# The down product of a spline-weight feed-forward layer: quarters of outputs, segment sums, and a reordered residual

## What is computed

```python
x = layernorm(x + attention(x))                    # 16 heads of 32, low-rank factors
x = layernorm(x + x * decayed_running_sum(ctx*ctx))
gate_w = spline(gate_cp, 2048, 512)                # cubic in 8134 control points,
up_w   = spline(up_cp, 2048, 512)                  # read out at out*in positions
down_w = spline(down_cp, 512, 2048)
inter = silu(x @ gate_w.T) * (x @ up_w.T)          # 2048 hidden units
x = layernorm(x + inter @ down_w.T)                # the down product
```

## Time and profile before

| | us |
|---|---|
| median of 3 runs (669.69 to 670.2) | 669.72 |
| the profiled execution | 670.12 |
| its span, first to last instruction | 668.3 |
| PE busy in it | 648.3 (97%) |
| feed-forward block 0, gate matmul to gate matmul (366.38 to 448.62) | 82.24 |
| blocks 1 and 2, each | 71.0 |
| from the last index' gate matmul to the end | 16.5 |

### The profile page before, as it was taken

How to read it: one execution, slowest core, us unless ns; L and a number is a source line. 1 busy time by engine, 2 the same in 40 slices (tenths; PEclk the granted TensorE clock), 3 DMA queues, 4 the chain that set the end, 5 groups by cost and what they waited for, 6 DMA issues and landing times.

```text
span 668.3 us, 12061 instructions
## 1 busy us (share of the span) xinstructions
PE 648.3 (97%) x4312; PEld 532.6 (80%) x4312; DVE 421.9 (63%) x790; ACT 360.5 (54%) x1038; POOL 291.5 (44%) x351
## 2 busy tenths in 40 slices
PE   8999999999999999999988799999999999999995
PEld 8687888878888788887856577888888888888884
DVE  3465686768777677776777788666554555454434
ACT  5566665656657676676776556552333333333222
POOL 0746389797747768585654936100010001000102
PEclk9999999999999999999998999999999999999998
DMA  9612020030220422021123662742183416440301
GB/s 328 225 59 96 1 95 1 2 127 1 60 99 2 137 75 69 7 74 43 42 66 71 157 166 69 209 104 46 32 232 78 100 32 184 92 103 0 127 1 63
DMA packets 22268, 58.07 MB, mean 87 GB/s; under 512 B 4033, under 2 KB 7233, under 8 KB 21313
## 3 DMA queue, kind: packets, MB, share of 16 engines
q1 hardware_dynamic: 17296, 45.50, 23.3%
q0 software_dynamic: 4624, 11.28, 5.6%
q10 hardware_dynamic: 288, 0.52, 0.3%
HBM read 32.11 MB, written 8.39 MB: 61 GB/s over the span
## 4 chain that ended last, share of the span: by engine, by line
PE 90%; DVE 4%; ACT 4%; issue 1%; POOL 0%; DVEq 0%; POOLq 0%; ACTq 0%
PE bank L303 22%; PE bank L305 21%; PE bank L304 21%; PE bank L490 8%; PE bank L478 5%; PE bank L512 5%; PE bank L1216 2%; PE bank L1121 2%; ACT probs L679 2%; PE bank L498 1%; PE bank L529 1%; PE bank L402 1%; PE bank L316 1%; PE bank L1190 1%; ACT hidden_hi_lo L1394 1%
## 5 line engine op out<-in xcount | busy, mean ns | idle before, releaser
L679 ACT ACTIVATE probs<-bank,minus_max 128x256 f32<-128x256 f32 x256 | 118.6, 488 | 38.8 <-DVE minus_max L847 38.6
L847 DVE TENSOR_REDUCE minus_max<-bank 128x2 f32<-128x512 f32 x128 | 79.5, 683 | 46.3 <-PE bank L478 46.3
L303 PE MATMUL bank<-down,hidden_hi_lo 128*128 128x512 f32 x256 | 100.8, 394 | 1.5 <-DVE hidden_hi_lo L1427 1.5
L304 PE MATMUL bank<-down,hidden_hi_lo 128*128 128x512 f32 x256 | 99.9, 390 | 0.0
L305 PE MATMUL bank<-down,hidden_hi_lo 128*128 128x512 f32 x256 | 99.8, 390 | 0.0
L1381 ACT ACTIVATE silu<-bank 128x512 f32<-128x512 f32 x64 | 38.3, 598 | 80.7 <-PE bank L305 79.9
L1423 DVE TENSOR_TENSOR hidden<-bank,silu 128x512 f32<-128x512 f32 x64 | 44.1, 690 | 59.5 <-PE bank L305 57.3
L858 DVE COPY probsT<-bank 128x512 f32<-128x512 f32 x96 | 59.9, 679 | 19.7 <-PE bank L490 19.6
L1427 DVE TENSOR_TENSOR hidden_hi_lo<-hidden,hidden_hi_lo 128x512 fp32r<-128x512 f32 x64 | 45.6, 712 | 40.8 <-ACT hidden_hi_lo L1394 40.7
L1394 ACT CAST hidden_hi_lo<-hidden 128x512 fp32r<-128x512 f32 x64 | 39.7, 621 | 52.7 <-DVE hidden L1423 52.7
L1498 POOL TENSOR_TENSOR ffn_var_eps<-ffn_mean_var,constants 128x4 f32<-128x4 f32 x3 | 0.6, 199 | 154.9 <-DVE ffn_mean_var L1443 154.9
(11 more groups left out here) (172 smaller groups left out, 1610.8 us busy)
## 6 DMA issues: line engine op xcount, KB each, us to landing
features_by_group<-features_by_cell SPq DMA_DIRECT2D x128, 128.0 KB, 2.3
ctx_squared_T<-in_ctxT SPq DMA_DIRECT2D x8, 512.0 KB, 6.2
xres<-in_x SPq DMA_DIRECT2D x8, 512.0 KB, 4.6
x_in<-x SPq DMA_DIRECT2D x16, 256.0 KB, 2.9
x_residual<-x POOLq DMA_DIRECT2D x4, 1024.0 KB, 6.7
xin_T<-in_xT SPq DMA_DIRECT2D x7, 512.0 KB, 4.0
x<-x_rows SPq DMA_DIRECT2D x7, 512.0 KB, 4.3
out_x<-x_residual POOLq DMA_DIRECT2D x12, 256.0 KB, 3.0
```

The source lines that it names most:

```text
L303: nc.tensor.matmul(out, wh, xh, start=first, stop=False)
L304: nc.tensor.matmul(out, wh, xl, start=False, stop=False)
L679: inc(nc.scalar.activation(probs[:, g, t, :], S[g][:, t * T:(t + 1) * T], ACT.Exp, bias=nmax[:, g, t:t + 1], accum_out=rsum[:, t, g:g + 1] ...
L847: inc(nc.vector.tensor_reduce(nmax[:, g, :], S[g][:].rearrange("p (t k) -> p t k", t=TT), AX.X, ALU.max, negate=True), "max")
```

## The change

Hidden units and outputs are both cut into Q = 4 quarters. A unit's position in every down row is its own number, so a unit lies close to the knots of some rows only. Quarters are chosen so that outside a quarter's own outputs the units can be joined to 16 segments that hold no knot of the other outputs' rows.

- `pe_raw`: the product of a quarter's 64 units of an index with its own 128 outputs, exactly. Two quarters lie on the partitions 0 to 63 and 64 to 127 of an index: six matmuls of 64 rows, in alternation into two banks. Results are now transposed: outputs on the partitions, 512 tokens as columns.
- `pe_moments`: two full matmuls for an index with the constant `by_segment` gather four moments of each segment into bank Mo. Twice in a block ACT and DVE split Mo into high and low, and `pe_polynomials` multiplies them with `down_by_moment` into all four banks (12 matmuls).
- One pair of units is moved between two quarters to make them equal; three more matmuls of 64 rows correct for it.
- `act_outs` and `dve_outs` copy the four banks out, `pe_outs` turns them back with 16 transposes, and the residual is added with 16 instructions for each pair of token tiles, because the residual's columns are sorted otherwise than those of the sum (`column_order`; x, context, Wo, decay and out_x are permuted on the host).
- A step is now two indices of a pair of quarters (st = 0 to 7); a feature group is used at st = g // 2 and again at 4 + g // 2. The turns, the jobs, the adds, and the statistics get new places; the norm goes from DVE to ACT (`act_out`) with its factors from POOL.
- The down jobs are 13 instead of 32, with 8 matmuls of 256 columns each instead of 2, ten of them in the first five indices of block 0. Their makers (426 KB with the mask, for each job) are rounded by two POOL DMAs from DRAM to DRAM in batches 2 and 3 and come in by 13 DMAs that SP issues, in four buffers.

```diff
+        k = i - 2 * NG
+        pe.wait_ge(s_mkd[k % 4], 16 * (k // 4 + 1))
+        mk = mk_dn[k % 4][:, 0:OUT_MAKER].rearrange("p (c h m) -> p c h m", c=2, h=2)
+        pieces = out[:].rearrange("p (e m) -> p e m", e=2)
+        if k == STEPS:
+            for piece in range(2):
+                for of, coef in ((0, 0), (1, piece)):
+                    for h in range(2):
+                        last = nc.tensor.matmul(out[:, piece * GROUP:piece * GROUP + P], mk[:, of, h, 0:P],
+                                                downD[:, h, coef, P:2 * P], start=of == h == 0, stop=of == h == 1)
+            inc(last, "w")
+            return
+        for cb in range(2):
+            for b in range(2):
+                q = 2 * (k // Q) + b if k < STEPS else 2 * ((k - STEPS - 1) % 2) + cb
+                for h in range(2):
+                    last = nc.tensor.matmul(pieces[:, :, cb * P:(cb + 1) * P], mk[:, cb, h, b * PART:b * PART + P],
...
+    def sp_makers_out(sp, k):
+        if k == 0:
+            sp.wait_ge(s["mkc"], 32)
+            sp.wait_ge(s["mkm"], 16)
+        if k < 3:
+            wait(sp, "v", 2 * B)
+        elif k == 3:
+            wait(sp, "o", 2 * B)
+        else:
+            wait(sp, "ws", 2 * NG + k - 3)
+        sp.dma_start(mk_dn[k % 4][:].bitcast(F32), makers_d2[k].bitcast(F32)).then_inc(s_mkd[k % 4], 16)
+
+    def pool_round_makers(pool, part):
+        at = slice(7 * part, min(7 * part + 7, DJOBS))
+        inc(pool.dma_start(makers_d2[at, :, 0:OUT_MAKER], makers_out_d[at, :, 0:OUT_MAKER]), "mkc", 16)
...
+    def pe_moments(pe, n, st, j):
+        pair, pr = divmod(st, Q)
+        pe.wait_ge(s["hl"], index(n, st, j) + 1)
+        if pr == j == 0:
+            wait(pe, "mol", 2 * n + pair)
+            if n == st == 0:
+                wait(pe, "ws", AHEAD_JOBS)
+                pe.wait_ge(s["seg"], 16)
+        for h in range(2):
+            last = nc.tensor.matmul(Mo[:], by_segment[:, JT * st + j, :], hid[:, st % 2, h, j, :],
+                                    start=pr == h == j == 0, stop=pr == Q - 1 and h == j == 1)
+        if pr == Q - 1 and j == 1:
+            inc(last, "mo")
...
+    def pe_raw(pe, n, st, j):
+        pair, pr = divmod(st, Q)
...
+        if pr == j == 0:
+            if n == pair == 0:
+                wait(pe, "r1", 2 * B)
+            elif n == 0:
+                pe.wait_ge(s["ws"], NJOB)
+            elif pair == 0:
+                wait(pe, "yqa", 2 * n - 1)
+                wait(pe, "yqd", 2 * n - 1)
+            else:
+                wait(pe, "add", 2 * n)
+        for k, (lo_w, lo_h) in enumerate(((0, 0), (0, 1), (1, 0))):
+            for b in range(2):
+                rows_ = slice(b * PART, (b + 1) * PART)
+                last = nc.tensor.matmul(Dn[2 * pair + b][:], raw[st][rows_, lo_w, j * P:(j + 1) * P],
+                                        hid[rows_, st % 2, lo_h, j, :], start=pr == j == k == 0, stop=False)
+        if st == MOVED_STEP and j == 0:
+            pe.wait_ge(s["hused"], index(n, st, j))
+            for lo_w, lo_h in ((0, 0), (0, 1), (1, 0)):
+                last = nc.tensor.matmul(Dn[1][:], raw[STEPS][0:PART, lo_w, 0:P], hid[0:PART, st % 2, lo_h, 0, :],
+                                        start=False, stop=False)
+        inc(last, "hused")
...
+    def pe_polynomials(pe, n, pair):
+        pe.wait_ge(s["mol"], 2 * n + pair + 1)
+        if n == 0:
+            wait(pe, "wld", STEPS + 2 * pair)
+        for q in range(Q):
+            last = three(Dn[q][:], [by_poly[:, pair, h, q * P:(q + 1) * P] for h in range(2)], [mom[:, pair, h, :] for h in range(2)],
+                         False, pair == 1)
+            inc(last, "d" if pair else "kap")
+
...
+
+    def pe_outs(pe, n, t):
...
-            wait(pe, "rs1", 2 * B)
-        elif g == 0:
-            wait(pe, "add", BT * (n - 1) + t + 1)
+            pe.wait_ge(s["yqa"], 2 * n + 2)
+            pe.wait_ge(s["yqd"], 2 * n + 2)
+        elif t == 2 and n < NB - 1:
+            pe.wait_ge(s["add"], 2 * n + 1)
+        for q in range(Q):
+            last = nc.tensor.transpose(Dn[outs_bank(n, t)][:, q * P:(q + 1) * P], yq[:, q, t * P:(t + 1) * P], ident[:])
+        inc(last, "pm")
...
+    def jobs_of(n, st, j):
+
+        first = AHEAD_JOBS + 2 * index(n, st, j)
+        return range(first, min(first + 2, NJOB)) if n == 0 else ()
+
...
+            pe_gate_up(pe, n, st, j)
+            pe_turn(pe, n, st, j, 0)
+            pe_fill(pe, n, st, j)
+            if n and st == 1 and j == 0:
+                pe_polynomials(pe, n - 1, 1)
+            if st:
+                pe_moments(pe, n, st - 1, j)
+                pe_raw(pe, n, st - 1, j)
+            elif n:
+                pe_moments(pe, n - 1, STEPS - 1, j)
+                pe_raw(pe, n - 1, STEPS - 1, j)
+            if st == 5 and j == 1:
+                pe_polynomials(pe, n, 0)
+            if n and (st, j) == (1, 1):
+                pe_outs(pe, n - 1, 0)
+                pe_outs(pe, n - 1, 1)
+            if n and (st, j) == (2, 1):
+                pe_outs(pe, n - 1, 2)
+                pe_outs(pe, n - 1, 3)
+            pe_turn(pe, n, st, j, 1)
+
...
+    def act_moments(act, n, pair):
+        act.wait_ge(s["mo"], 2 * n + pair + 1)
+        wait(act, "d" if pair else "kap", Q * n)
+        inc(nc.scalar.copy(mom[:, pair, 0, :], Mo[:]), "moh")
+
+    def act_outs(act, n, q):
+        act.wait_ge(s["d"], Q * n + q + 1)
+        wait(act, "pm", BT * n)
+        inc(nc.scalar.copy(yq[:, q, :], Dn[q][:]), "yqa")
+
+    def act_out(act, n, t):
+        act.wait_ge(s["nm"], BT * n + t + 1)
+        inc(nc.scalar.activation(res[:, t, :], res[:, t, :], ACT.Identity, bias=fnm[:, t:t + 1], scale=frstd[:, t:t + 1]), "yout")
...
+            act_hh(act, n, st, j)
+            for i in jobs:
+                act_job(act, i, job_bank(i))
+            for i in jobs:
+                act_job_hi(act, i)
+            if n and (st, j) == (1, 0):
+                act_outs(act, n - 1, 0)
+                act_outs(act, n - 1, 2)
+            if n and st in (5, 6):
+                act_out(act, n - 1, 2 * (st - 5) + j)
+            act_turn(act, n, st, j, 1)
+
...
+    def dve_add(dve, n, pair, part):
+        if pair == part == 0:
             dve.wait_ge(s["fres"], 16 * n + 16)
-        dve.wait_ge(s["d"], BT * n + t + 1)
-        inc(nc.vector.tensor_tensor(res[:, t, :], Dn[t][:], res[:, t, :], ALU.add), "add")
+        dve.wait_ge(s["pm"], BT * n + 2 * pair + 2)
+        b = outs_bank(n, 2 * pair)
+        for i in range(8 * part, 8 * part + 8):
+            at, to, size_ = RUNS[i]
+            o = res[:, 2 * pair:2 * pair + 2, to:to + size_]
+            last = nc.vector.tensor_tensor(o, banks[:, b:b + 2, at:at + size_], o, ALU.add)
+        if part:
...
+                continue
+            if (st, j) == (1, 0):
+                dve_outs(dve, n - 1, 1)
+                dve_outs(dve, n - 1, 3)
+            elif st == 2:
+                dve_add(dve, n - 1, 0, j)
+            elif st == 3:
+                dve_add(dve, n - 1, 1, j)
+            elif (st, j) == (4, 0):
+                dve_out_stats(dve, n - 1, 0)
+            elif (st, j) == (4, 1):
+                dve_out_stats(dve, n - 1, 1)
+                dve_out_stats(dve, n - 1, 2)
+            elif (st, j) == (5, 0):
+                dve_out_stats(dve, n - 1, 3)
+                dve_out_aggr(dve, n - 1)
...
+        pool.wait_ge(s["rstd"], n + 1)
+        for t in range(BT):
+            inc(nc.gpsimd.tensor_scalar(fnm[:, t:t + 1], fmv[:, t, 0:1], frstd[:, t:t + 1], -1.0, ALU.mult, ALU.mult), "nm")
...
                     sp_features(sp, 0, g, c)
-            sp_store(sp, B - 2)
+            for k in range(3, 7):
+                sp_makers_out(sp, k)
             for t in range(2):
                 sp_x2in(sp, 1, t)
             for c in range(CELLS):
+                if c < 3:
+                    sp_makers_out(sp, 2 * c + 7)
+                    sp_makers_out(sp, 2 * c + 8)
                 for g in range(QUAD, NG):
                     sp_features(sp, 0, g, c)
+            sp_store(sp, B - 2)
```

More of the change, by code:

```diff
@@ L1 @@
+import math
 import numpy as np
@@ new lines, in column_order, with I_of, split12 @@
+def column_order():
+    _, frac, knot = knots()
+    outs = quarters(frac, knot)[0]
+    order, runs, used = [], [], [0] * Q
+    for c in range(CELLS):
+        for q in range(Q):
+            here = [int(o) for o in outs[q] if o // P == c]
+            runs.append((q * P + used[q], len(order), len(here)))
+            used[q] += len(here)
+            order += here
+    return np.array(order), runs
+def I_of(o, c):
+    return ((o * INTER + c * P) * (NC - 1)) // (NS - 1)
+def split12(v):
+    m, e = np.frexp(v)
+    high = np.ldexp(np.round(m * 4096) / 4096, e)
+    return high, v - high
@@ new lines, in spline_tables @@
+    units = [int(u) for u in perm[MOVED_GROUP, P:2 * P]]
+    for u in moved:
+        i, c = units.index(u), u // P
```

(34 more changed lines are left out.)

590 lines of the change are left out of this document (305 added, 285 removed).

## The result

| | us |
|---|---|
| before, median (range) | 669.75 (669.69 to 670.2) |
| after, median (range) | 663.05 (662.14 to 664.47) |
| ratio after/before | 0.9899, 95% interval 0.9887 to 0.9912 |
| predicted | 637.5 (620 to 657) |
| profiled execution of after, its span | 662.71, 660.9 |

The account below looks back on a forecast made before the run. PE's matmul streaming was taken to bound the kernel. From 670.12 us: +1.4 gate start, -12.4 block 0, -21.0 blocks 1 and 2, -9.3 block 3, +8.0 end, +1.0 clock gave 637.8, median 637.5; range 620 to 657.

Parts of the forecast that it names:

- a change between full and partial rows costs extra ... 0.10: PE, each index: entering and leaving partial-row matmuls costs 0.10 us each, two per index, 0.20 of 2.69 us.
- once more waits for makers, features: Block 0: further PE waits for transfers, sixth index at 401.0; block 12.4 us less, with -0/+5 for transfers.
- The stand for the makers: Block 0: PE stands from 369.2 to 374.6 us until the fourth job's makers land.
- the clock at 1.0 for all stands: A PE stand of 5 us can bring the clock down; 1.0 us added to the sum.
- the pairs side by side: `pe_raw`: two 64-row matmuls run together in 0.227 us, so three pairs cost 0.68 us an index.
- gate's start: Ahead of block 0: two of three longer jobs are exposed, so gate starts 1.4 us later, at 367.8.
- the three waits of PE for `x_residual`: `pe_outs` for the second tile pair waits for additions: 2.2 us in blocks 1 and 2, 2.5 in block 3.
- the additions in a row: DVE's small residual additions of 64 columns on average are 0.13 us apart; eight take 1.05 us.
- the end: After the last index's matmuls: serial down, split, transposes, additions and statistics take 20.4 us, 8.0 more than before.
- Statistics and `act_out`: At (4,1) and (5,0), ACT waiting for POOL's factors holds `silu` back: 1.6 us for each of three blocks.
- the second: Rival: weight loads of a pair run one after the other, 28.7 us more less 5 of stalls: 661 us; 4%.
- The third: Rival: DVE and DMA set more: additions at 0.22 (+7), makers later, POOL held by its DMA: 648 to 660 us; 17%.

Follow-up runs that it names:

- raw128: Changed kernel with the six 64-row raw matmuls of an index made three 128-row ones, outputs not the reference's: 650.48 us, ratio 0.9711.
- ungrouped: best2 with the raw matmuls back behind each index, so rows change four times in a step: 643.66 us, ratio 0.9608.
- best2: Changed kernel with raw matmuls grouped per step, SP's store, makers and down jobs later, finer feature waits, second-pair output transposes one index later: 634.66 us, ratio 0.9475.
- best3: best2 with SP's x_in for the third tile of block 1 ahead of the makers of steps 3 to 6, store behind: 627.21 us, ratio 0.9367.

## Why the prediction was wrong

**The step that failed first: "a change between full and partial rows costs extra ... 0.10".** I compared the one step into the scores and the one out of them with the usual pace and stopped there. The next step is late by as much. The bound "0 and 0.10" had no room for it. An index was 2.93 and not 2.69, 0.24 for each of the 59 indices behind the first five: +14.2. Of the 0.24, 0.20 are the two second steps; `raw128` (0.44 less an index) and `ungrouped` against `best2` (0.20 for a change) show it. The other 0.04 is left open.

**The step that failed second: the transfers of "once more waits for makers, features", -0/+5.** The stand for the makers was right in place and length (to 374.0; forecast 374.6). But I let the two jobs behind it run at the full clock. They ran at half:

```profile
374.00 3.90 PE L1294 MATMUL bank<-spline_coef_T_down,makers_out 128*128 128x256 f32 x16 [4.78 <-DMA makers_out<-makers_rounded]
```

The forecast had 1.92 for them. The window of that stretch has the granted clock at 0.50:

```profile
374.00:377.90 3.90, 3.90 (x17) 3.82 (x18) 0.45 (x1) 0.37 (x1) 3.08 (x2) 0.50 0.96 346
```

Then the features of the second half, issued between makers until 397.2, held PE by 5.7 us at 396.2, again followed by half clock. The sixth index started at 409.5, not 401.0: +8.5. I had booked the clock at 1.0 for all stands.

**Not seen at all: block 1's queue.** +4.8 there beside the changes of rows. The change leaves SP's store where it was, ahead of the second half of the features. What it moved are both ends of the wait: the store became ready 35 us later, behind DVE's statistics and POOL's norm, and the features are due at index 4 instead of 8. The faster PE had no part in it: the kernel before reaches its own index 4 after 16.3 us of the block, the changed one after 16.9, its wait left out. I argued with care what each moved DMA would be late for, and looked neither at what a DMA that stays waits for, nor at when the features in block 1 are first read.

**Right:** the pairs side by side (`raw128` aside, 0.23 apart in all runs); gate's start; the three waits of PE for `x_residual` (1.7 to 1.9; forecast 2.2 to 2.5); the additions in a row, by the line below; nothing gained or lost before 353.6 us; the end, 24.4 us from the last gate matmul for a forecast of 2.7 + 20.4 = 23.1, where 0.2 is the change of rows. Statistics and `act_out` cost about 0.7 and not 1.6 (the index at (5,0) took 4.07 instead of 3.38).

```profile
475.21 1.14 DVE L1664 TENSOR_TENSOR x_residual<-bank,x_residual 128x68 f32<-128x68 f32 x8
```

Each addition lasts 0.22, so the eight are (1.14 - 0.22) / 7 = 0.13 apart, as forecast from instructions in a row. The 0.19 in the forecast is an estimate from the cycles that the Trainium skill (VectorE: DVE Perf Modes, The TRN2 errata) gives. It is near the length of one addition, and no run here shows it as the distance in a row. The forecast's two prices for dearer additions don't agree with each other: 7 us for 0.09 more each counts some 80 additions, 3.6 us for 0.06 more only 60. Neither entered the sum.

**The rivals.** The time of the second, 661, is the nearest to 663.05. It came from weight loads one after the other within a pair, and the pairs are 0.23 apart; loads are late here too, but at the change between heights. The third, 648 to 660, is half true by its heading ("DVE and DMA set more of it"), and SP's long row of issues ahead of the third step, which spoke for it, did hold PE in block 0. But none of the three parts that made its sum was at work: the additions were not 0.22, the makers not later, POOL not held (0.86 and 0.83 us for its two DMAs). A time that fits is no proof of a mechanism.

Beyond the forecast: with the queue put in order and the changes halved the same idea gives 627.2, 10 us under what I had predicted for it.

## What to carry to other kernels

When matmuls of another height are mixed in, price the change by two steps behind it, not one, and put the matmuls of one height together: the same work in another order was worth 3.1 us a block here where PE had no other wait, and 7 to 9 us of the time. When a change reorders the work, or makes the engine that sets the pace faster, go through every transfer on every queue, those that the change leaves alone too: when is what it waits for ready now, and when is it first read? One item that waits for a slow engine holds all that is ready behind it. A total that gives half of the expected gain may be a full gain with a new wait behind it: read the index, not the sum.

## What the runs showed of the hardware

- A change between 128 and 64 rows, or 32 and 128, costs TensorE 0.20 us each way, in two steps of 0.10; no weight load was drawn ahead over the changes that were read (in `after` at 501.09 and 501.98).
- In after the stands of PE of 4.8, 5.7 and 3.9 us each came with a stretch of 6.8 us at 1.2 GHz that began within the stand, and the one of 1.7 us at 541.4 was followed by 3.4 us of it. The equal stand of 1.7 us at 478.9 and the one of 1.9 us at 604.0 were followed by none. By an estimate from these rows (work at half the clock takes twice as long) the stand at 541.4 cost twice its length, the three long ones about one and a half times. In `best3` one of 3.6 us in block 0 was followed by 3.4 us. Which stands bring the clock down, and for how long, is left open.
- SP needs 0.64 us for each feature copy (32 rows of 4 KB) and 0.32 to 0.68 for makers of 128 rows of 3.3 KB. 32 copies a block are 20 us of issue; that is why 16 copies that become ready together are late by 10 us. Whether fewer, taller copies would be issued faster was not tried.
